# Attention beside an FP4 gated layer on one core: the maxima of a round turned by VectorE and stored by GpSimd

## The reference

```python
xn = _layernorm(x)
qkv = xn @ Wqkv.T                       # q, k, v: 16 heads of 16 channels
dots = einsum('bhid,bhjd->bhij', q, k) * dh ** -0.5
dots = where(causal_mask, -inf, dots)
attn = softmax(dots)                    # needs the maximum of each row of dots
out = einsum('bhij,bhjd->bhid', attn, v) @ Wout.T + bout
h = silu(fp4_linear(xn, w_gate)) * fp4_linear(xn, w_up)
return x + out + fp4_linear(h, w_down)
```

## Time and profile before

| | us |
|---|---|
| median of three runs | 2815.54 |
| profiled execution | 2811.82 |
| its span | 2810.2 |
| PE busy | 2577.6 (92%) |
| ACT busy | 2034.4 (72%) |
| DVE busy | 1936.9 (69%) |
| POOL busy | 687.3 (24%) |
| maximum stage, DVE L744 | 702.3 in 1536 reductions |
| maximum stage, ACT L723 | 640.5 in 1536 activations |
| maximum stage, PE L676 | 489.9 and 492.1 in 1536 each |

### The profile page before, as it was taken

One profiled execution on the slowest core, in us unless ns is written; L12 is line 12 of the kernel. 1 busy time (PEld: TensorE's weight loads), 2 busy tenths in 40 slices (PEclk: granted clock), 3 DMA queues, 4 the chain that ended last, 5 costly groups with the idle time before them and its releaser, 6 DMA issues.

```text
span 2810.2 us, 60356 instructions
## 1 busy us (share of the span) xinstructions
PE 2577.6 (92%) x18236; PEld 1313.6 (47%) x18236; DVE 1936.9 (69%) x5533; ACT 2034.4 (72%) x3510; POOL 687.3 (24%) x478
## 2 busy tenths in 40 slices
PE   2995998898889859999999999999999999999999
PEld 1883444444444424444454445445444445444445
DVE  6895998898889865656655665655566564656555
ACT  1554887897889857777766777775777775777775
POOL 3563233323232212111111211211121121212211
PEclk8997999999999989999999999999999999999999
DMA  2785544444454442122123022031221231220200
GB/s 68 234 269 119 78 61 67 69 67 69 67 70 67 62 78 45 32 33 46 28 63 72 22 41 47 22 69 58 33 49 26 34 69 54 45 47 22 41 24 31
DMA packets 117099, 175.52 MB, mean 62 GB/s; under 512 B 24880, under 2 KB 93232, under 8 KB 116272
## 3 DMA queue, kind: packets, MB, share of 16 engines
q1 hardware_dynamic: 97392, 147.33, 27.9%
q10 hardware_dynamic: 16576, 15.73, 2.1%
q0 software_dynamic: 2816, 8.91, 1.1%
HBM read 129.37 MB, written 42.53 MB: 61 GB/s over the span
## 4 chain that ended last, share of the span: by engine, by line
PE 53%; ACT 4%; issue 4%; DMA 1%; SPq 1%; DVE 0%; ACTq 0%; POOL 0%; DVEq 0%; POOLq 0%
PE O L918 17%; PE S L902 15%; PE F L938 10%; PE F L978 5%; ACT probs L1047 4%; PE F L968 2%; PE S L989 2%; PE S L905 2%; SPq L528 1%; PE F L931 1%; DMA y<-in_L_attn_x_dram 1%; DMA q_st<-s_shift 0%; ACTq L1042 0%; DVE o_turned L1253 0%; DVE ht_lo L1241 0%
## 5 line engine op out<-in xcount | busy, mean ns | idle before, releaser
L1047 ACT ACTIVATE probs<-S 128x1024 f32<-128x1024 f32 (+3 forms) x1280 | 1074.7, 897 | 213.7 <-PE S L902 77.3
L744 DVE CUSTOM_DVE_ANT_0 m_excess<-m_S,m_excess 128x512 f32<-128x512 f32 (+7 forms) x1536 | 702.3, 531 | 58.8 <-ACT m_excess L723 38.3
L723 ACT ACTIVATE m_excess<-m_DIFF 128x512 f32<-128x512 f32 (+7 forms) x1536 | 640.5, 473 | 124.8 <-PE m_DIFF L676 36.1
L902 PE MATMUL S<-q_st,k_st 128*128 128x512 bf16 (+3 forms) x2560 | 648.3, 351 | 65.7 <-DMA q_st<-s_shift 28.7
L918 PE MATMUL O<-probs,v_sb 128*32 128x512 f32 (+3 forms) x5120 | 602.3, 542 | 1.7 <-POOL v_sb L1124 1.7
L676 PE MATMUL m_DIFF<-m_k,m_q_diff 128*128 128x512 bf16 (+7 forms) x1536 | 489.9, 326 | 61.0 <-DMA m_q_diff<-s_q 29.8
L676 PE MATMUL m_S<-m_k,m_q 128*128 128x512 bf16 (+7 forms) x1536 | 492.1, 330 | 18.5 <-DVE m_row_max L744 10.6
L902 PEld LDWEIGHTS S<-q_st,k_st 128*128 128x128 bf16 x2560 | 213.4, 98 | 407.8 <-ACT probs L1047 236.3
L631 POOL TENSOR_TENSOR m_q_diff<-m_zero,m_q 48x4096 bf16<-48x4096 bf16 x32 | 224.3, 7011 | 519.6 <-DMA m_q<-s_q 508.5
L676 PEld LDWEIGHTS m_S<-m_k,m_q 128*128 128x128 bf16 x1536 | 150.4, 98 | 257.5 <-DVE m_row_max L744 181.3
L1241 DVE TENSOR_TENSOR ht_lo<-F,ht_hi 128x512 fp32r<-128x512 f32 (+1 forms) x128 | 71.0, 558 | 232.0 <-ACT ht_hi L1062 232.0
(11 more groups left out here) (163 smaller groups left out, 4167.9 us busy)
## 6 DMA issues: line engine op xcount, KB each, us to landing
k_st<-s_k SPq DMA_DIRECT2D x96, 256.0 KB, 8.5
q_st<-s_q SPq DMA_DIRECT2D x384, 64.0 KB
s_q<-a_part SPq DMA_DIRECT2D x48, 256.0 KB, 3.0
s_k<-a_part SPq DMA_DIRECT2D x48, 256.0 KB, 2.2
m_q<-s_q SPq DMA_DIRECT2D x96, 128.0 KB, 3.6
m_k<-s_k SPq DMA_DIRECT2D x96, 128.0 KB, 6.4
m_q_diff<-s_q SPq DMA_DIRECT2D x96, 128.0 KB, 7.9
m_k<-s_k SPq DMA_DIRECT2D x96, 124.0 KB, 5.1
```

The source lines that it names most:

```text
L723: act.activation(excess[u % MAX_EXCESS][:, 0:keys // 2], DIFF[u % MAX_BUFS][:, 0:keys // 2], ACT.Relu) \
L744: dve.tensor_tensor_reduce(larger, S[u % MAX_BUFS][:, 0:keys // 2], larger, 1.0, -3e38, ALU.add, ALU.max, column).then_inc(reduced[u % MAX ...
L902: ins = pe.matmul(S[half][:, s % 2, 0:st.width], k_st[p][:, s, st.j * P:(st.j + 1) * P], q_st[st.c % 2][:, s, st.skip:QC], start=True, sto ...
L1047: act.activation(probs[half][st.n % 2][:, :, 0:st.width], S[half][:, :, 0:st.width], ACT.Exp, scale=SCALE).then_inc(exped[half], 1)
```

## The change

The block transpose of DVE takes the place of PE's transpose. It turns each 32 x 32 block of the 128 x 128 maxima in itself: what was at row a * 32 + s and column c * 32 + r is then at row a * 32 + r and column c * 32 + s. So the rows are not in the order of the DRAM tensor, and the store puts this right with its addresses. POOL negates, rounds to the first part and subtracts for the second part, all in SBUF, and stores each part in four DMAs, one for each 32 rows, in runs of 32 elements (64 bytes). PE and ACT have nothing left to do at a round's end; PE's wait at the fourth difference goes, and so does ACT's for the store. DVE has two new waits: for its own transpose before it goes on, and, before the transpose, for POOL's negation of the round before. On POOL the whole of this stands in `store`, at its old place behind the negation of the next round's first two loads.

```diff
-        shift_part = [sb(f"m_part{k}", [MAX_HEADS * NKB, P], BF16) for k in range(SHIFT_PARTS)]
+        row_turned, minus_max = sb("m_row_turned", [P, P]), sb("m_minus_max", [P, P])
+        shift_part = [sb(f"m_part{k}", [P, P], BF16) for k in range(SHIFT_PARTS)]
-        turn = DIFF[MAX_BUFS - 1][0:MAX_HEADS * NKB, 0:P]
...
-            def store(n):
+            def store(n, negates):
+                for p in range(2):
+                    pool.wait_ge(q_negated[p], negates + PRIMED)
+                pool.wait_ge(turned, n + 1 + PRIMED)
+                pool.tensor_tensor(minus_max[:, :], zero[:, 0:1].to_broadcast([P, P]), row_turned[:, :], ALU.subtract) \
+                    .then_inc(negated, 1)
+                pool.wait_ge(negated, n + 1 + PRIMED)
+                pool.sem_inc(aside, 1)
+                pool.tensor_copy(shift_part[0][:, :], minus_max[:, :]).then_inc(part0, 1)
+                pool.wait_ge(part0, n + 1 + PRIMED)
+                pool.tensor_tensor(shift_part[1][:, :], minus_max[:, :], shift_part[0][:, :], ALU.subtract).then_inc(part1, 1)
                 pool.wait_ge(part1, n + 1 + PRIMED)
                 for k in range(SHIFT_PARTS):
-                    pool.dma_start(dram["shift"][k, bass.ds(n * MAX_HEADS, MAX_HEADS), :]
-                                   .rearrange("h (i t) -> (h i) t", t=P), shift_part[k][:, :]).then_inc(shift_st, 16)
-                pool.wait_ge(shift_st, n * (16 * SHIFT_PARTS) + 16 * SHIFT_PARTS)
-                pool.sem_inc(stored, 1)
+                    rows = dram["shift"][k, bass.ds(n * MAX_HEADS, MAX_HEADS), :].rearrange("h (i t) -> (h i) t", t=P)
+                    for a in range(P // SLOT):
+                        at = slice(a * SLOT, (a + 1) * SLOT)
+                        pool.dma_start(rows[:, at].rearrange("(c r) s -> r c s", r=SLOT),
+                                       shift_part[k][at, :].rearrange("r (c s) -> r c s", s=SLOT)).then_inc(shift_st, 16)
+                pool.wait_ge(shift_st, n * (16 * shift_dmas) + 16 * shift_dmas)
...
-                if u == MAX_BUFS - 1:
-                    pe.wait_ge(part1, n + PRIMED)
...
-                    pe.wait_ge(joined, n + 1 + PRIMED)
-                    pe.transpose(turn, row_max[:, :, :].rearrange("p h i -> p (h i)"), ident[:, :]).then_inc(turned, 1)
...
-                    act.wait_ge(turned, n + 1 + PRIMED)
-                    act.wait_ge(stored, n + PRIMED)
-                    act.activation(shift_part[0][:, :], turn, ACT.Copy, scale=-1.0).then_inc(part0, 1)
...
-                    dve.wait_ge(part0, n + 1 + PRIMED)
-                    dve.scalar_tensor_tensor(out=shift_part[1][:, :], in0=turn, scalar=-1.0, in1=shift_part[0][:, :],
-                                             op0=ALU.mult, op1=ALU.subtract).then_inc(part1, 1)
+                    dve.wait_ge(joined, n + 1 + PRIMED)
+                    dve.wait_ge(negated, n + PRIMED)
+                    dve.transpose(row_turned[:, :], row_max[:, :, :].rearrange("p h i -> p (h i)")).then_inc(turned, 1)
+                    dve.wait_ge(turned, n + 1 + PRIMED)
```

More of the change, by code:

```diff
@@ L593, in shift_phase @@
         scored, reduced = sems("m_scored", MAX_BUFS), sems("m_reduced", MAX_EXCESS)
-        joined, turned, part0, part1, stored, shift_st = (
-            sem("m_joined"), sem("m_turned"), sem("m_part0"), sem("m_part1"), sem("m_stored"), once("m_st"))
+        joined, turned, negated, part0, part1, shift_st = (
+            sem("m_joined"), sem("m_turned"), sem("m_negated"), sem("m_part0"), sem("m_part1"), once("m_st"))
+        shift_dmas = SHIFT_PARTS * (P // SLOT)
         aside = once("m_aside")
@@ L649, in _ @@
                     negate(n + 1, load)
-                store(n)
+                store(n, loads_before(n + 1, 1) + 1)
             for load in range(2, loads):
                 negate(B * rounds - 1, load)
-            store(B * rounds - 1)
+            store(B * rounds - 1, loads_before(B * rounds, 0))
         @block.sync
```

## The result

The changed kernel takes 2821.99 us (median of 13 runs, 2816.73 to 2824.6); the kernel before 2815.15 us (13 runs, 2810.2 to 2817.19). The ratio is 1.0023, 95% interval 1.0014 to 1.0032: some 6.5 us slower, 3.9 to 9.0. A gain of 7.4 us was forecast. The profiled execution has a span of 2817.2 us against 2810.2.

What follows compares the result with a forecast made beforehand. DVE was taken to bound the maximum stage. Seven boundaries at 1.4 + 0.3 = 1.7 us win 11.9, the last round's end loses 4.5: -7.4, giving 2808.1 us; own range 2803 to 2812, overall 2794 to 2822.

Steps and rivals of the forecast that it cites:

- That DVE has a stall of its own: Round's end: DVE stands at its own back branch (5.4 to 5.8 us) and keeps such a stall after the change.
- The label "waits for ACT": Rival, round's end: DVE stood for ACT; 8.0 of 8.5 us go, 56 won less 4.5, 2764 us; chance 0.03.
- That the load's traffic makes the branch dear: Round's end: branch time depends on SP's 12 load DMAs; 2.6 us away from such a load.
- What the branch then costs: I take 1.4: DVE's branch at each round's end: branching 0.5 us earlier wins 1.4 us, between bounds of nothing and 3.7.
- plain shift: Rival, round's end: the branch keeps its 6 us; 0.5 + 0.3 won per boundary, 2814.4 us; chance 0.27.
- The slope: ACT's branch in two rounds: 0.28 us earlier gave return 1.5 us earlier; would give DVE's 0.5 us over 2 us.
- Restart: I take 0.3 won: DVE's first units after a round's end: 0.3 us won per boundary, bounds +0.7 and -0.3.
- The four ready units: Start of a round: four scored units stand ready when DVE restarts, some 1.6 us of DVE work.
- The last round's end: 4.5: After the last join, waiting for the store to land: 4.5 us lost, bounds +3.5 and +6.0.
- the 0.4 added for the short runs: Last round's stores: the sum gave +4.1 us; 4.5 was put because they write runs of 64 bytes.
- POOL between the rounds: Pool's three operations and eight DMAs, about 8 us, fit in its 23.5 us idle stretch.
- slower: Rival, round's end: earlier branch wins nothing, PE's cold clock loses 0.3 per boundary, tail 4.5 to 6.0; 2823 us; chance 0.14.

Runs made afterwards that it cites:

- e1: Changed kernel, with SP's load at a round's end held until DVE has begun the next round: 2798.64 us, 0.9945 of the kernel before.
- e2: Kernel before, with SP's load at a round's end held until DVE has begun the next round: 2796.07 us, 0.9929 of the kernel before.
- e9: Changed kernel, with PE making the difference product of each round's seventh unit 22 times more: 2815.22 us, one run.
- e7: Changed kernel, with PE making the difference product of each round's seventh unit ten times more: 2820.11 us, one run.

## Why the prediction was wrong, step by step

**That DVE has a stall of its own** was right: 7.25 us remain of 7.8 with PE and ACT freed, ACT's branch costs 2.6 us, and its Relu is back at +0.3. The label "waits for ACT" would have promised 51.5 us. **That the load's traffic makes the branch dear** was right, and e1 and e2 show it in both kernels. The Trainium skill (Runtime: NRT & Kernel Launch, Instruction fetch mechanics) says that a taken branch to code outside the engine's window of two pages has to wait for a DMA of the target page. The traces agree: at every round's end DVE goes on 1.3 to 2.0 us after an 8 KB packet of the instruction queue has landed, and it is this packet that comes late behind the load.

**"What the branch then costs: I take 1.4"** failed. DVE branched 0.3 to 0.5 us earlier, 0.43 on average, at +0.83 and +0.99; 0.5 was worked out (the transpose took 0.311 us against 0.31). But 0.55 us were won at the restart, near the plain shift, not 1.4. The packet with DVE's code began 3.1 us behind the branch (mean of seven) where it had begun 3.3 behind it: asking earlier did not get it past the load. The slope came from ACT's two rounds and was carried over to DVE. In the kernel before, ACT was back at +5.1 and +5.3 in the two rounds in which it branched at +0.85, and at +5.7 to +6.5 in the five in which it branched at +0.98 or later; DVE was back at +7.25 to +7.46 wherever it branched between +1.18 and +1.49. DVE's own two kinds of branch, which cost the same 6 us, stood in the same rows and said so. In the changed kernel the rounds with the inner branch restart at 6.84 to 6.96, those with the outer at 7.47 to 8.06, 0.5 to 1.2 us later for a branch 0.15 us later; with the load held (e1) they are 0.2 to 0.5 apart. With the outer branch the packet began 3.1 to 3.7 us behind it, with the inner 2.9 to 3.0; why stays open.

**"Restart: I take 0.3 won"** failed in sign: 0.33 lost (excess 0.71 to 1.04). The four ready units carried DVE for 1.6 us, as said, but PE had been idle until after DVE's restart, and the clock stayed at 0.50 for 4.5 us from that restart on (mean of seven), where it had been 3.3 in the kernel before; e9 shows that with the clock up the excess is gone. Per boundary 0.22 won (0.55 less 0.33), 1.6 us in seven, where 11.9 were forecast.

**"The last round's end: 4.5"** was mis-sized: 8.1. Its sum up to the landing was right to 0.1 us (+4.1), with parts that were off by up to 0.3 and cancelled (DVE to POOL 0.17 instead of 0.3, POOL's operations with their handovers 1.66 instead of 1.4, eight issues 0.54 apart, landing 1.7 instead of 1.9), so the 0.4 added for the short runs was not needed. Missing was a term that no line of the sum had: the drain of POOL, 1.37 us before and 5.29 after, +3.9. It was in the trace of before, on the sequencer's line L571, between a landing at 1024.4 and a main phase that begins at 1027.79, and I ended the sum at the landing.

**POOL between the rounds** is hidden, as forecast: the second and third load of every round take 21.87 us, and PE never waits for POOL's negation between the rounds. The nearest rival was "slower" (2823, chance 0.14): its clock loss of 0.3 was met, its branch that wins nothing was not quite so, and its tail of 4.5 to 6.0 was too short for the same missing term. That its number is so near the measured one is in part luck: it lost 2.1 us between the rounds where 1.6 were won, and was short by 2.1 to 3.6 at the end. With 8.1 for the tail the plain shift, too, comes out slower: 2815.5 - 5.6 + 8.1 = 2818.0, and with the 1.6 us measured between the rounds 2822.0.

## What to carry to other kernels

A wait put down to another engine, or to nobody, at a loop's end may be the waiting engine's own branch: read the sequencer's branch and the instruction behind it, and keep large loads out of that moment (here that alone won 0.7% with one semaphore). Work moved onto POOL as many small DMAs is paid again when a phase closes with a drain; count the phase's DMAs, not the last round's. Before freeing an engine that feeds the bound one, ask what it does in the time it now stands idle: PE came back at half clock.

## What was not expected of the hardware

- POOL's drain at the end of a phase took 1.37, 2.67, 5.13 and 5.29 us after 16, 32, 56 and 64 small DMAs issued by POOL, whether the last was 2 us or 80 us old and in rows of 64 or 256 bytes, and 1.4 us after 16 of 512 KB. What it does in that time stays open.
- The same branch cost DVE 2.7 to 3.0 us with the DMA queues quiet and 5.5 to 7.1 us with one load of 12 DMAs under way; the difference goes with one 8 KB packet of instructions, which began 0.9 to 1.2 us behind the branch in the one case and 2.6 to 4.3 in the other.
- PE had been idle from 448.67 to 452.80 between two busy stretches, and its granted clock fell only at 453.95, 1.15 us after it had begun to work again (e7). Behind such a fall DVE lost 0.3 to 0.4 us for each pair of units made at the lower clock (e7: idle for 0.30 and 0.23 us before the reductions at 552.19 and 553.40).
